# Selective scan of a twelve-layer decoder: the inputs' end put together, outputs in the states' block, one branch for the stepwise scan, x added to from PSUM

## What is computed

```python
def step(h, inp):
    dt_t, B_t, C_t, u_t = inp
    dA = jnp.exp(jnp.clip(dt_t[:, :, None] * A, -20.0, 0.0))
    dB_u = jnp.clip(dt_t[:, :, None] * B_t[:, None, :] * u_t[:, :, None], -10.0, 10.0)
    h = jnp.clip(h * dA + dB_u, -100.0, 100.0)
    y = jnp.einsum('bdn,bn->bd', h, C_t)
    return (h, y)
...
# around it: x is layer-normalised; W_in gives the channels and a gate; a causal convolution of 4 taps and silu make u;
# W_x gives one raw step size and B, C; dt = clip(softplus(raw * W_dt + b_dt), 1e-4, 10); A = -exp(min(A_log, 5));
# y is layer-normalised, u * D is added, it is multiplied by silu(gate) and by W_out, and added to x
```

## Time and profile before

| | |
|---|---|
| time, median of 3 runs | 2736.97 us (2731.4 to 2741.11) |
| profiled execution | 2736.85 us, its span 2735.1 us |
| PE, PEld, DVE, ACT, POOL busy | 78%, 49%, 63%, 44%, 23% of the span |
| granted TensorE clock, mean | 0.885 of full speed |

### The profile page before, as it was taken

The page is one execution under the profiler, slowest core; times in us unless marked ns, Lnnn a source line. Parts: engine busy times, 40 slices in busy tenths (PEclk is TensorE's granted clock), DMA queues, the critical chain, the costliest instruction groups (busy, mean ns, idle before and its releaser), DMA issues. The chain is left out here.

```text
span 2735.1 us, 28267 instructions
## 1 busy us (share of the span) xinstructions
PE 2138.7 (78%) x10151; PEld 1331.9 (49%) x10181; DVE 1711.1 (63%) x2529; ACT 1200.4 (44%) x1900; POOL 618.9 (23%) x349
## 2 busy tenths in 40 slices
PE   5799898794699979889392888888758989372985
PEld 3455566682233336768231444444535654252575
DVE  5555455326667845422474999999635766857665
ACT  2344322101366744311155999999713236302340
POOL 3321122121322110022214656565000210000100
PEclk8899999697899989789696999999869989696895
DMA  6562210343954000224210000000111000000001
GB/s 129 85 90 28 96 56 20 113 160 100 126 75 66 7 21 1 93 90 148 59 46 15 1 1 1 1 1 1 62 59 35 0 1 0 0 8 20 0 1 37
DMA packets 107529, 126.74 MB, mean 46 GB/s; under 512 B 14823, under 2 KB 98676, under 8 KB 106357
## 3 DMA queue, kind: packets, MB, share of 16 engines
q1 hardware_dynamic: 94404, 109.63, 17.4%
q10 hardware_dynamic: 10098, 7.71, 1.0%
q0 software_dynamic: 2880, 7.48, 0.8%
HBM read 91.11 MB, written 33.29 MB: 45 GB/s over the span
## 5 line engine op out<-in xcount | busy, mean ns | idle before, releaser
L3191 DVE TENSOR_TENSOR_SCAN l2s_h<-l2s_aw 128x2048 f32<-128x2048 f32 x64 | 290.3, 4536 | 5.1 <-ACT l2s_rs L3236 3.4
L3150 PE MATMUL l2s_big<-g_xn,g_ident 128*128 128x512 f32 x512 | 259.4, 609 | 11.5 <-ACT g_xn L3229 6.3
L3205 POOL TENSOR_SCALAR l2s_aw<-l2s_aw 128x2048 f32<-128x2048 f32 x64 | 212.7, 3323 | 10.3 <-DVE l2s_aw L3183 5.1
L591 DVE TENSOR_REDUCE l1at_nm<-l1at_s 128x1 f32<-128x512 f32 x256 | 162.2, 684 | 67.1 <-PE l1at_s L441 66.2
L3142 PE MATMUL l2s_c_ps<-g_ident,l2s_h 128*128 128x128 f32 x1024 | 149.3, 279 | 54.9 <-ACT g_xn L3229 36.0
L3142 PEld LDWEIGHTS l2s_c_ps<-g_ident,l2s_h 128*128 128x128 f32 x1024 | 117.6, 142 | 146.2 <-issue 87.5
L691 ACT ACTIVATE g_xn<-l1at_s 128x512 f32<-128x512 f32 x256 | 143.6, 598 | 84.4 <-PE l1at_s L465 83.7
L3229 ACT ACTIVATE g_xn<-l2s_c_ps,l2s_ct 128x512 f32<-128x512 f32 x256 | 162.9, 688 | 18.0 <-PE l2s_c_ps L3142 17.8
L3222 ACT ACTIVATE l2s_aw<-l2s_dt,l2s_A 128x2048 f32<-128x2048 f32 x64 | 128.2, 2004 | 0.0
L591 DVE TENSOR_REDUCE l0at_nm<-l0at_s 128x2 f32<-128x384 f32 x128 | 69.7, 557 | 88.7 <-PE l0at_s L441 87.3
L3150 PEld LDWEIGHTS l2s_big<-g_xn,g_ident 128*128 128x128 f32 x512 | 82.3, 191 | 81.7 <-ACT g_xn L3229 58.8
(11 more groups left out here) (875 smaller groups left out, 4940.2 us busy)
## 6 DMA issues: line engine op xcount, KB each, us to landing
l1f_w<-in_L_ffn_w_dram SPq DMA_DIRECT2D x16, 1024.0 KB, 8.1
l0f_w<-L_ffn_experts_inter_dram SPq DMA_DIRECT2D x7, 1024.0 KB, 5.2
l0f_w<-n_L_ffn_experts_out_dram SPq DMA_DIRECT2D x7, 1024.0 KB, 9.7
l0at_qs<-l0at_parts SPq DMA_DIRECT2D x18, 256.0 KB, 9.0
l0at_ks<-l0at_parts SPq DMA_DIRECT2D x18, 256.0 KB, 17.1
l1at_qs<-l1at_parts SPq DMA_DIRECT2D x18, 256.0 KB, 9.1
l1at_ks<-l1at_parts SPq DMA_DIRECT2D x18, 256.0 KB, 20.7
expert_rows<-g_zeros SPq DMA_DIRECT2D x1, 4096.0 KB, 12.8
```

What stands on the lines that cost most here:

```text
L591: V.tensor_reduce(nm[:, s % 2, qts[0]:qts[-1] + 1, r], s1[:, u % 3, 0:len(qts) * KEYS].rearrange("p (q k) -> p q k", k=KEYS), AX, ALU.max, ...
L3150: nc.tensor.matmul(acc[:, tb, :], ident[:], hCT[:, tb, :], start=n == 0, stop=n == NST - 1).then_inc(acc_done, 1)
L3191: V.tensor_tensor_scan(out=h_all[:, i % 2].rearrange("p c t -> p (c t)"), data0=dA[:, i % 2].rearrange("p c t -> p (c t)"), data1=wd[:, i ...
L3205: nc.gpsimd.tensor_scalar(wd[:, i % 3], wd[:, i % 3], 10.0, -10.0, ALU.min, ALU.max).then_inc(clipped, 1)
```

## The change

- **Loads and selector.** A new class `ScanParts` holds the tiles that the layer shares: the block `aw`, `sel`, `cols`, `conv_w`, `A`. Its scope (l2w, a "holder") spans L1's cross attention, L1's mixture and the scan. GpSimd makes `sel` in the cross attention's main block. SyncE issues the 12 loads in the mixture, behind the last expert's weights, raw weights going into parts of `aw`. The blocks 2 are gone; memsets and A go to the start of `scan_inputs`.
- **Inputs' end.** The clamp of dt goes from GpSimd to VectorE, behind each addition; the exponentials of batches 1 and 2 go behind `take_rows(3)`, all three logarithms to the end; the product dt * u of batch 0 goes from the scan's start to the inputs.
- **Outputs in the states' block.** `scan_close` is gone; its programs follow the scan's in `scan_fast`. Statistics cover batches 0 to 2 first, then 3. Two gates are loaded as soon as the last scan is done. `norm(0)` and `skip(0)` stand ahead of the branch.
- **One branch.** The flag is made there too. Every engine reads it once: if set, it goes through the stepwise inputs, states and outputs (their programs are collected by `Later` and separated by meetings), else through the rest of the outputs.
- **x from PSUM.** VectorE adds each half batch of the output projection to x from PSUM and takes x's statistics at once, instead of ScalarE's copies, the addition of 4096 columns and the next layer's statistics.

```diff
+class ScanParts:
+    def make_rows(self, pool):
+        ch.step(self.nc.gpsimd.memset(sel[:], 0.0))
+        for n in range(3):
+            ch.step(self.nc.gpsimd.affine_select(out=sel[:], in_=sel[:], compare_op=ALU.not_equal, fill=1.0, base=-2 * nst * n,
...
+    def load(self, sp):
+            for dst, src in loads:
+                sp.dma_start(dst, src).then_inc(self.loaded, 16)
...
@@ mixture, SyncE
                 for e in range(2, n_exp):
                     sp.wait_ge(y_ready, CTL * (e - 1))
                     weights(sp, e)
+                if scan is not None:
+                    scan.load(sp)
                 for u in range(2):
                     sp.wait_ge(put[u], 16 * CTL * len(range(u, n_exp, 2)))
...
+                if scan is not None:
+                    scan.wait_loaded(sp)
@@ scan_inputs
+            dve.wait_ge(dt_ready, b + 1)
+            V.tensor_scalar(to, to, 1e-4, 10.0, ALU.max, ALU.min).then_inc(dt_kept, 1)
...
-        @block.gpsimd
-        def _(pool):
-            def program():
-                for b in range(BATCH):
-                    pool.wait_ge(dt_ready, b + 1)
-                    nc.gpsimd.tensor_scalar(dt[:, b], dt[:, b], 1e-4, 10.0, ALU.max, ALU.min).then_inc(dt_kept, 1)
...
+                take_rows(b)
+                if last:
+                    exponentials((1, 2), 4)
...
+            exponentials((3,), 7)
+            logarithms((1, 2, 3), 8)
@@ scan_fast
+    def decide(eng, engine, finish):
+        eng.wait_ge(flag_ready, 1)
+        found = eng.value_load(flag[0:1, 0:1], min_val=0, max_val=1)
+        with eng.If(found != 0):
+            exact_scan(eng, engine)
...
+        with eng.If(found == 0):
+            finish()
...
+        def add(b, half):
+            t = b * QT + 2 * half
+            dve.wait_ge(delta_ready, 2 * b + half + 1)
+            V.tensor_tensor(x[:, t:t + 2, :], x[:, t:t + 2, :], d_ps[:, half, :].rearrange("p (t n) -> p t n", n=DM), ALU.add).then_inc(x_added, 1)
...
+        def finish():
+            for b in range(BATCH):
+                mix(b)
+                if b:
+                    add(b - 1, 0)
+                    add(b - 1, 1)
+                    take_stats(b - 1, 0)
+                    take_stats(b - 1, 1)
```

More of the change, by code:

```diff
@@ new lines, in _, with program @@
+    @block.gpsimd
+    def _(pool):
+        def program():
+            pool.sem_inc(hC_ready, 2)
+            with pool.Fori(0, BATCH) as b:
+                for n in range(NST):
+                    pool.wait_ge(c_copied, b * NST + (n + 3))
+                    pool.wait_ge(h_ready, b * NST + (n + 1))
+                    nc.gpsimd.tensor_tensor(dA[:, n % 3], h_all[:, n % 2], c_sb[:, n % 2, None, :].to_broadcast(WIDE),
+                                            ALU.mult).then_inc(hC_ready, 1)
+        program()
@@ L3363, in _ @@
             norm(2)
+            skip(2)
+            act.wait_ge(stats_ready, 2)
+            norm(3)
             skip(3)
-            norm(3)
-            for b in range(BATCH):
-                copy_out(b)
-        @block.sync
-        def _(sp):
-            for b in range(BATCH):
-                if b >= 2:
-                    sp.wait_ge(gated, b - 1)
-                sp.dma_start(gate[:, b % 2], gate_dram[b]).then_inc((gate_even, gate_odd)[b % 2], 16)
-def scan_outputs(G, nc, c, T, ps, w, hmax, gate_dram, dims, exact, run):
+        root(0)
@@ new lines, in _, with load_gate, finish @@
+        act.wait_ge(stats_ready, 1)
+        norm(0)
+        skip(0)
+        root(1)
+        decide(act, "scalar", finish)
+    @block.sync
+    def _(sp):
+        def load_gate(b):
+            sp.dma_start(gate[:, b % 2], gate_dram[b]).then_inc((gate_even, gate_odd)[b % 2], 16)
+        def finish():
+            for b in range(2, BATCH):
+                sp.wait_ge(gated, b - 1)
+                load_gate(b)
+        sp.wait_ge(h_ready, N)
+        load_gate(0)
+        load_gate(1)
+        sp.wait_ge(gate_even, 16)
+        sp.wait_ge(gate_odd, 16)
+        decide(sp, "sync", finish)
@@ new lines, in _, with square, root, copy_out @@
+    @block.scalar
+    def _(act):
+        E = nc.scalar
+        def square(b):
+            act.wait_ge(centred, b + 2)
+            if not (isinstance(b, int) and b == 0):
+                act.wait_ge(var_ready, b)
+            act.sem_inc(taken, 1)
+            E.activation(sq, at(y_all, b), ACT.Square).then_inc(sq_ready, 1)
+        def root(b):
+            act.wait_ge(v_ready, b + 2)
+            E.activation(rs[:], rs[:], ACT.Sqrt).then_inc(std_ready, 1)
+        def copy_out(b):
+            for q in range(QT):
+                act.wait_ge(delta_ready, b * QT + (q + 2))
+                E.copy(xn[:, b * QT + q, :], big[:, q, 0:DM]).then_inc(delta_copied, 1)
+        def first(b):
+            square(b)
+            root(b)
+        def both(b):
+            square(b + 1)
+            root(b + 1)
+            copy_out(b)
+        def program():
+            act.sem_inc(delta_copied, 4)
+            batches(act, first, both, copy_out)
+        program()
```

1299 lines of the change are left out of this document (648 added, 651 removed).

## The result

The changed kernel takes 2668.46 us, median of 6 runs (2665.88 to 2671.22), beside 2734.95 (2731.4 to 2741.11) for the kernel before on the same chip: a ratio of 0.9747, 95% interval 0.9731 to 0.9762. It is faster, as forecast with 0.96, but faster than the forecast's range allowed: 2680.4 was the number, 2672 the lower end. The forecast also started from 2736.97, the median of the first three runs of the kernel before; over six it is 2734.95, so 2.0 us of the distance between 2680.4 and 2668.46 come from the start and not from the gain. Run again later, it took 2670.71 (2668.48 to 2675.5) against 2734.22, ratio 0.9772 (0.9752 to 0.9792).

A forecast was written before the change was run, and what follows sets the result against it. The prediction took the engine that is last at each of five seams in one layer as the bound; 23.4 + 12.2 + 1.3 + 19.7 = 56.6 us off 2736.97 gave 2680.4, range 2672 to 2690.

The forecast's parts named there:

- The front: Normalisation to PE's first projection: earlier loads and no selector or memset block there save 23.4 us (22.1 to 24.7).
- I can't say which: 1345.4: Normalisation's last copy of x: 1344.1 or 1346.7 depending on PE's clock, taken as 1345.4, against 1351.45 before.
- The selector in the cross attention: GpSimd making the selector in L1's narrow cross attention: taken to cost VectorE 0 us.
- Rival B: L1's narrow cross attention: GpSimd's selector holds VectorE for 15.3 us, giving 2696; chance 0.05.
- rival E: Front: the loads come late or it gains less, at most 9.5 us, giving 2690; chance 0.04.
- The inputs' end and the states' start: Step-size clamp on VectorE with ScalarE reordered saves 12.2 us (9 to 16); moving batch 0's product saves 1.3.
- The outputs: Last scan to the next layer: the next layer starts at 1995.8 instead of 2015.5, saving 19.7 us.
- D: Outputs: every engine's time to read the flag and branch over the stepwise code, taken as 3.5 us (0.8 to 4.9).
- Rival C: Outputs: VectorE becomes the bound, a batch 9.2 us against PE's 8.8, giving 2685; chance 0.08.
- Rival A: Branch in the outputs: the jump grows with the code passed, 8.4 us more on all engines, giving 2689; chance 0.10.
- Rival D: Scan loop: its 6.96 us iterations get slower, 2751 us in total at 1.1 more each; chance 0.02.
- so a sum over the profile can be taken from either: Whole kernel: the profiled 2736.85 us and the timed median 2736.97 agree, so either can start the sum.

The follow-up runs named there:

- selector back: Changed kernel with the selector made by GpSimd in a block of its own behind the normalisation again: 2689.62 us.
- x added as a whole: Changed kernel with ScalarE copying the output projection, VectorE adding all 4096 columns to x at the end, and no statistics of x taken: 2673.77 us.
- no branch: Changed kernel without the flag's reading, the branch and the stepwise fallback behind it: 2668.3 us.

## Why the prediction was right in direction and too high

**What bounds the kernel, and which seams give: right.** All of what is gained in this layer lies at the seams named. The convolutions, the projections between them and the 64 iterations kept their time (72.16; 436.61 against 436.82).

**The front, 23.4 against 26.87: the mechanism right, the size off.** The steps hold one by one: reciprocal, tiles, PE's turns at once, no late loads, no block of the selector, no GpSimd instruction between mixture and scan. This is the step of the sum that failed. It did so twice: at "I can't say which: 1345.4", where I took the middle of two clocks for the last copy, and at PE's start as the end of the count. The copies ended as at the high clock (12.0 us behind the block's start where 12.4 was my number for it, and 13.7 stood in the sum), so PE began 12.4 behind it where I had 14.0. And the first projection, for which I held 1.8 us ready in the range alone, ran at the high clock too, in all ten profiles whose front was not edited. These two are 1.7 and 1.8 us, 3.5 in all; selector back, where PE idles for 17 us ahead of it, brings the second one back. Put back singly, selector and loads make 17.71 + 7.36 = 25.1 of the 26.87; the other 1.8 (the block of memsets among them) no run edits.

**The selector in the cross attention: right at 0.** VectorE's longest group in that block while GpSimd makes the selector:

```profile
L1432 DVE TENSOR_REDUCE l1x_negmax<-l1x_s_ps 128x16 f32<-128x1024 f32 x4 | 4.9, 1222 | 16.3 <-PE l1x_s_ps L1369 16.3
```

It was 1222 ns before, too. Rival B did not occur. **The late loads** (rival E) did not occur: SyncE issued the twelve in 14 us, before the experts were done, the first and the last of them:

```profile
1279.92 0.58 SPq L2718 DMA_DIRECT2D l2w_aw<-in_L_attn_W_in_dram  x1
...
1293.42 0.51 SPq L2718 DMA_DIRECT2D l2w_cols<-in_L_attn_ln_b_dram  x1
```

**The inputs' end and the states' start, 13.5 against 14.65: right.** VectorE's clamp took 1.23 us (1.216 was the row), and the last one ended at 1448.25, where my chain gives 1475.3, less the 26.4 us by which this kernel is ahead there, 1448.9. What the prediction did not see is that its own chain contained a loss: it costed the regrouping and the clamp as one, and 1.30 us of it were given away.

**The outputs, 19.7 against 21.13 and 18.68: right.** D was 3.8 to 3.9 where I took 3.5; batch 0 was gated 25.88 us behind the last scan, 25.8 by my sum. PE's 32.15 us came out between 31.39 and 33.67, with the granted clock (1.00 and 0.93 at these two ends). Rival C, VectorE as the bound, did not occur: PE has no gap, and x added as a whole leaves PE as it was. Rival A would have made D 11.9. Rival D did not occur: the period is 6.82 us. Of the 21.13, x added as a whole shows 3.58; no run puts the end of the states' block, the order of the statistics or the three skipped blocks back, so the rest of this gain is read from the rows and not from an edit.

**What made the range miss.** 2680.4 lies 11.9 us above 2668.46. Of that 2.0 is the median of the kernel before, from which the sum started. The stretches up to the next layer sum to 62.4 us in the first profile, 5.8 more than the forecast's 56.6, and 3.5 of that is the front. The remaining 4.1, up to the measured gain of 66.5, lie outside the layer. The step that failed there is "so a sum over the profile can be taken from either": I held my range by the unknown costs of the edits alone and took the unchanged stages as fixed. They are not. Their start moved between 1326.18 and 1335.89, and the rest was 711 to 722 us, in kernels whose program there is the same. The range was narrow by its own terms too: the bounds listed for it add up to 8.8 us down (2671.6) and 5.7 up, not to 2674 and 2685. A second set of runs gave 2670.71, still 1.3 below 2672, so some 2 us of the first result are scatter; the miss is not.

Where the rest's 8.6 us lie, a split of it shows. Up to L3's cross attention it took 517.65 us against 519.87 before (517.1 to 520.7 in all fourteen profiles). Then come that cross attention, and the normalisation and routing of L3's mixture; each row has the stretch, its length and PE's busy time in it, and the granted clock third from the end. Before:

```profile
2535.30:2672.50 137.20, 118.75 (x607) 82.07 (x607) 91.36 (x168) 47.96 (x67) 9.79 (x5) 0.92 0.00 1
2672.50:2713.30 40.80, 22.30 (x101) 21.23 (x101) 17.24 (x62) 4.18 (x10) 0.57 (x3) 0.50 0.03 10
```

The changed kernel:

```profile
2470.70:2605.70 135.00, 115.19 (x606) 80.65 (x606) 92.03 (x168) 47.88 (x67) 9.82 (x5) 0.93 0.00 1
2605.70:2642.30 36.60, 18.04 (x100) 17.10 (x100) 17.24 (x61) 4.18 (x10) 0.58 (x3) 0.59 0.04 11
```

The cross attention takes 134.2 to 144.6 us in the twelve profiles with the new layer, and that is most of the rest's scatter. The routing takes 40.8 in both profiles with the old layer, at 1.2 GHz throughout, and 35.7 to 36.9 in eleven of the twelve others; in the twelfth, no branch, it is 40.4 at 1.2 GHz again. So 2.2, 2.2 and 4.2 us of the 8.6 lie in these three stretches, the last two with the granted clock, and the low clock of the last one occurs with the new layer as well. The rest is 719.7 in the two profiles with the old layer and 716.3 on average in the twelve with the new one. Whether the change has a part in that, through where the clock falls, stays open.

## What to carry to other kernels

Cut the profile at marks that both kernels have, and give each stretch its own scatter: a change of 1 us is plain in a stretch without TensorE's clock in it, and lost in the total. Where a block without PE work is removed, count the lower clock of PE's next stretch with it (1.8 us here beside the block's own 15.9). A gain just ahead of other PE work need not arrive in full: of 3.6 us in no branch, 2.3 did. When a wait moves from one engine to another, cost the edits of that seam one by one: here the change's order of ScalarE's functions cost 1.3 us beside the order of before, and another order gained 7.
